# One accumulating DMA of two products in the first three rows of taps, with twelve product buffers

## The reference

```python
# layer 0: deformable attention, 8 heads, 4 points, 8 channels a head, q = x as tokens
v = q @ W_value + b_value
off = q @ W_off + b_off                       # per pixel, head and point: (dx, dy)
attn = softmax(q @ W_attn + b_attn)           # over the 4 points
# each point samples v bilinearly at (pixel position + off) of its own pixel
out = (sampled * attn).sum(points) @ W_out + b_out + q
# layer 1: binary 3x3 convolution of sign(x + move0), sign weights with a scale per channel,
# batch norm over the batch, + x, + move1, PReLU, + move2
```

## Time and profile before

| | |
|---|---|
| median of 3 runs | 95.57 us (95.44 to 96.04) |
| the profiled execution | 95.7 us |
| its span in the trace | 93.9 us |
| PE busy in the span | 76.6 us (82%) |
| DVE, POOL, ACT busy | 65.0, 51.0, 47.9 us |
| granted TensorE clock, mean | 0.953 |

### The profile page before, as it was taken

The page is one execution under the profiler, slowest core; times in us unless marked ns, Lnnn a source line. Parts: engine busy times, 40 slices in busy tenths (PEclk is TensorE's granted clock), DMA queues, the critical chain, the costliest instruction groups (busy, mean ns, idle before and its releaser), DMA issues.

```text
span 93.9 us, 1689 instructions
## 1 busy us (share of the span) xinstructions
PE 76.6 (82%) x648; PEld 33.0 (35%) x648; DVE 65.0 (69%) x81; ACT 47.9 (51%) x76; POOL 51.0 (54%) x47
## 2 busy tenths in 40 slices
PE   5999799879999999999997799999999999220000
PEld 4547074112246544333331355333333345010000
DVE  2624695995999664987973954997776408659930
ACT  2200899988689990399708950220000039419900
POOL 7920000059999999999998568899800000005000
PEclk9999999999999999999999999999999999996555
DMA  1998000000083083470924700910910000000095
GB/s 27 249 358 327 6 0 0 0 0 7 0 168 56 0 168 63 82 141 0 178 49 84 143 7 3 194 30 0 195 35 0 0 7 0 0 0 0 14 257 180
DMA packets 3209, 7.10 MB, mean 76 GB/s; under 512 B 512, under 2 KB 1024, under 8 KB 3200
## 3 DMA queue, kind: packets, MB, share of 16 engines
q0 software_dynamic: 1008, 3.67, 20.6%
q1 hardware_dynamic: 1904, 2.89, 9.8%
q10 hardware_dynamic: 288, 0.43, 1.5%
HBM read 2.27 MB, written 1.05 MB: 35 GB/s over the span
## 4 chain that ended last, share of the span: by engine, by line
PE 67%; ACT 15%; DVE 7%; issue 4%; POOL 3%; ACTq 1%; DVEq 0%; POOLq 0%
PE banks L431 27%; PE banks L451 23%; PE banks L444 4%; ACT tab L609 3%; ACT hat L614 3%; PE banks L483 3%; PE banks L501 3%; POOL ap L754 2%; ACT prod L734 2%; PE banks L404 2%; PE banks L396 2%; ACT prod L736 2%; DVE bns L957 1%; ACT sg L680 1%; ACT u L602 1%
## 5 line engine op out<-in xcount | busy, mean ns | idle before, releaser
L754 POOL TENSOR_TENSOR ap<-ays,hat 128x512 f32<-128x512 f32 x30 | 40.4, 1564 | 17.4 <-ACT ays L623 15.7
L850 DVE TENSOR_TENSOR prod<-banks,vpad 128x1024 f32<-128x1024 f32 (+1 forms) x33 | 38.6, 1187 | 11.7 <-PE banks L431 11.7
L431 PE MATMUL banks<-ap,cst 64*64 64x512 f32 x240 | 33.9, 596 | 1.3 <-DVE prod L850 1.1
L451 PE MATMUL banks<-prod,wo 64*64 64x512 f32 x200 | 27.8, 590 | 0.0
L431 PEld LDWEIGHTS banks<-ap,cst 64*64 64x64 f32 x240 | 10.1, 132 | 17.2 <-issue 9.4
L451 PEld LDWEIGHTS banks<-prod,wo 64*64 64x64 f32 x200 | 9.9, 133 | 11.5 <-issue 9.6
L779 POOL TENSOR_SCALAR prod<-prod,prm,st 128x512 f32<-128x512 f32 x2 | 1.5, 768 | 17.7 <-ACT st L728 17.7
L623 ACT ACTIVATE ays<-banks 128x512 f32<-128x512 f32 x8 | 4.7, 588 | 9.9 <-DVE banks L822 9.9
L609 ACT ACTIVATE tab<-u,cst 128x1024 f32<-128x1024 f32 x8 | 8.9, 1141 | 0.2
L680 ACT ACTIVATE sg<-banks,st 128x512 bf16<-128x512 f32 x2 | 1.3, 687 | 14.9 <-PE banks L451 14.9
L614 ACT ACTIVATE hat<-tab 128x1024 f32<-128x1024 f32 x8 | 8.3, 1050 | 0.1
(11 more groups left out here) (81 smaller groups left out, 74.0 us busy)
## 6 DMA issues: line engine op xcount, KB each, us to landing
prod<-prod POOLq DMA_DIRECT2D x7, 512.0 KB, 4.8
xs<-x_dram SPq DMA_DIRECT2D x3, 256.0 KB, 4.9
out_dram<-prod SPq DMA_DIRECT2D x4, 128.0 KB, 2.6
out_dram<-prod SPq DMA_DIRECT2D x2, 256.0 KB, 2.6
wcf<-w_conv_dram SPq DMA_DIRECT2D x1, 288.0 KB, 5.2
wab<-w_abs_dram SPq DMA_DIRECT2D x1, 288.0 KB, 5.2
xs<-x_dram ACTq DMA_DIRECT2D x1, 256.0 KB, 4.1
cst<-const_dram SPq DMA_DIRECT2D x1, 227.0 KB, 5.0
```

The lines of the kernel that those rows point to most:

```text
L431: mm = pe.matmul(ps_w[t % 2][rows_out, g, :], sel_of(g)[rows_in, rows_out], weights_at(t)[rows_in], start=True, stop=True)
L451: mm = pe.matmul(ps_out[g][rows_out], wo[rows_in, rows_in], source[rows_in, g, :], start=False, stop=last, skip_group_check=True)
L754: pool.tensor_tensor(ap[:, j % RAP, :], ays[:, t // TAPS % RY, :], hat[:, yh, 0, kx, :], ALU.mult).then_inc(s_ap, 1)
L850: nc.vector.tensor_tensor(by_half_row(prod[:, t % PR, g, :]), by_half_row(ps_w[t % 2][:, g, :]), v_window(g, yh, ky, kx), ALU.mult).then_i ...
```

## The change

In rows 0, 1 and 2 (`SUMMED_WHOLE`) one DMA now adds the two products of columns 2 and 3 onto those of columns 0 and 1: two slots of the ring onto two slots, 8 KB in each partition, 1 MB in all. It stands in POOL's list after weight 4(n+1)+3 and waits for product 4n+3. PE projects two units for such a row, both sums. Rows 3 to 6 keep their DMA of 512 KB and their three units, row 7 its four, so there are 3 x 2 + 4 x 3 + 4 = 22 units. The ring has PR = 12 buffers. `s_s2` has four semaphores, one for each row modulo 4. Where each unit is projected is written out in `UNITS_AT`.

```diff
--- before.py
+++ after.py
@@ -35,6 +35,7 @@
 
 ROWS = YH * TAPS
 SUMMED = range(ROWS - 1)
+SUMMED_WHOLE = range(3)
 DVE_COLUMNS = [2] + [0] * (ROWS - 1)
 GPSIMD_LINES = (0, 1)
 ORDER = (1, 0, 2, 3)
@@ -138,7 +139,7 @@
         RA, RAP = 3, 4
         a = sb("a", [P, RA, HALF])
         ap = sb("ap", [P, RAP, HALF])
-        PR = 8
+        PR = 12
         prod = sb("prod", [P, PR, G, HALF])
         over_sum = sb("over", [P, 2 * YH])
         overt = sb("overt", [P, 2, HALF])
@@ -209,7 +210,7 @@
         s_ap = sem("gpsimd_tap_weights_ready")
         s_w = sem("spread_ready")
         s_p = sem("products_ready")
-        s_s2 = [sem("even_pair_sums_ready"), sem("odd_pair_sums_ready")]
+        s_s2 = [sem(f"sums_ready{k}") for k in range(4)]
         s_acc = sem("units_projected")
         s_ov1 = sem("over_abs")
         s_ov = sem("over_ready")
@@ -323,20 +324,25 @@
 
             return t + 1 + (g if t == NT * YH - 1 else 0)
 
-        def units_of(n):
-
-            first = TAPS * n
-            if n == ROWS - 1:
-                return [("tap", t) for t in range(first, first + TAPS)]
-            return [("tap", first + 2), ("tap", first + 3), ("sum", n)]
-
-        UNITS_AFTER = {6: [("tap", 2), ("tap", 3)], 7: [("sum", 0)], 17: [("tap", 15), ("sum", 3)], 18: [], 20: [],
-                       21: [("tap", 18), ("tap", 19)], 31: [("tap", 28), ("tap", 29)]}
-        for n in range(2, ROWS):
-            for column in range(3):
-                UNITS_AFTER.setdefault(TAPS * n + column, units_of(n - 1)[column:column + 1])
-        UNITS = [unit for n in range(ROWS) for unit in units_of(n)]
-        UPPER_UNITS = sum(len(units_of(n)) for n in range(TAPS))
+        def sums_of(n):
+
+            return 2 if n in SUMMED_WHOLE else 1
+
+        def unit_of(t):
+
+            n, column = divmod(t, TAPS)
+            return ("sum", t) if n in SUMMED and column < sums_of(n) else ("tap", t)
+
+        def is_added(t):
+
+            n, column = divmod(t, TAPS)
+            return n in SUMMED and sums_of(n) <= column < 2 * sums_of(n)
+
+        UNITS_AT = {9: [0], 10: [1], 13: [4], 14: [5], 16: [14], 17: [15, 8], 18: [9, 12], 21: [18, 19], 22: [16], 24: [22],
+                    25: [23], 26: [20], 28: [26], 29: [27], 30: [24], 31: [28, 29]}
+        UNITS_AFTER = {t: [unit_of(k) for k in UNITS_AT[t]] for t in UNITS_AT}
+        UNITS = [unit for t in sorted(UNITS_AFTER) for unit in UNITS_AFTER[t]] + [unit_of(30), unit_of(31)]
+        UPPER_UNITS = UNITS.index(unit_of(12)) + 1
 
         def units_done(unit, g=G - 1):
 
@@ -462,11 +468,11 @@
                     pe.wait_ge(s_carry, 2)
                 last = unit in (UNITS[UPPER_UNITS - 1], UNITS[-1])
                 if kind == "sum":
-                    pe.wait_ge(s_s2[n % 2], 16 * (n // 2 + 1))
-                    source = prod[:, TAPS * n % PR]
+                    row = n // TAPS
+                    pe.wait_ge(s_s2[row % 4], 16 * (row // 4 + 1))
                 else:
                     pe.wait_ge(s_p, products_done(n, 0))
-                    source = prod[:, n % PR]
+                source = prod[:, n % PR]
                 mm = project_image(source, 0, last)
                 if unit == UNITS[-1]:
                     mm.then_inc(s_acc, 1)
@@ -755,16 +761,17 @@
 
             def pair_sum(n):
 
-                t = TAPS * n
-                pool.wait_ge(s_p, products_done(t + 1, G - 1))
-                pool.dma_start(prod[:, t % PR], prod[:, (t + 1) % PR], accum_op=ALU.add).then_inc(s_s2[n % 2], 16)
+                k = sums_of(n)
+                into = TAPS * n % PR
+                pool.wait_ge(s_p, products_done(TAPS * n + 2 * k - 1, G - 1))
+                pool.dma_start(prod[:, into:into + k], prod[:, into + k:into + 2 * k], accum_op=ALU.add).then_inc(s_s2[n % 4], 16)
 
             weight(2)
             weight(3)
             for n in range(ROWS - 1):
                 for column in range(TAPS):
                     weight(TAPS * (n + 1) + column)
-                    if column == 1:
+                    if column == 2 * sums_of(n) - 1:
                         pair_sum(n)
                 if n == 0:
                     pool.wait_ge(s_rec, 2)
@@ -836,14 +843,11 @@
                     dve.wait_ge(s_vlow, 2)
                 if t >= PR:
                     old = t - PR
-                    if old // TAPS in SUMMED and old % TAPS < 2:
+                    if is_added(old):
                         n = old // TAPS
-                        if old % TAPS == 0:
-                            dve.wait_ge(s_acc, units_done(("sum", n)))
-                        else:
-                            dve.wait_ge(s_s2[n % 2], 16 * (n // 2 + 1))
+                        dve.wait_ge(s_s2[n % 4], 16 * (n // 4 + 1))
                     else:
-                        dve.wait_ge(s_acc, units_done(("tap", old)))
+                        dve.wait_ge(s_acc, units_done(unit_of(old)))
                 dve.wait_ge(s_w, t + 1)
                 both = slice(0, G)
                 for g in ([both] if t < NT * YH - 1 else [slice(g, g + 1) for g in range(G)]):
```

## The result

The changed kernel is slower: 97.80 us, the median of 4 executions (97.38 to 98.92), against 95.50 us for the kernel before; the ratio is 1.021 [1.018, 1.024]. The forecast was 96.3 us, and its range ended at 97.6. The profiled execution takes 97.66 us with a span of 95.9 us, against 95.7 and 93.9, so 2.0 us have to be found. Executions more than 1.5% slower than the fastest of their kernel count in no ratio.

What follows compares the result with a forecast made beforehand. PE was taken as the bound, POOL hardly behind; 2.6 us from three units and 1.4 from the hole and smaller gaps stood against 4.6 of waits, 0.7 later unrounded: 96.3 us from 95.57, range 94.9 to 97.6.

Steps and rivals of the forecast that it cites:

- Case A: PE waits for the larger DMA at sums 0 and 4 (1.6 and 0.6 us), giving 96.3 us; chance 0.62.
- the hole at spread 20: PE stood 1.07 us waiting for product 18; hiding that product behind sums 9 and 12 would close it.
- The doubling of the data phase: A second 512 KB adds 2.75 us at 189 GB/s, so 1 MB lands 7.25 us after issue.
- B: Second half of the transfer nearly free, 2.65 us at 396 GB/s: 94.1 us, or 94.7 by the skill's fit; chance together 0.13.
- C: POOL's hold per DMA grows with bytes, 1.8 us not 0.9, delaying weights and later DMAs: 97.2 to 98.1 us; chance 0.18.
- D: PE, half busy from 28.7 to 34.6 us, falls to half clock, 1.7 us a block: 98 to 100 us; chance 0.04.
- the DMA of row 3 ... its data go behind those of row 2 (47.3) and land at 50.4: Row 3's DMA, issued at 43.3, queues behind row 2's and lands before sum 12 needs it at 51.2.
- both landings had under 1 us to spare: Rows 2 and 3 land at 47.7 and 50.4, sums 8 and 12 come at 48.6 and 51.2; slower DMAs delay the end.
- the twelve buffers cost nothing: The larger product ring is worth nothing, as each product's slot is free several us before it is needed.
- Forecast 0.7: Spread 20 starts at 52.9 instead of 52.19, so the kernel ends 0.7 us later.
- three units with 2.6 us: Three units removed from PE ahead of spread 20, 0.86 us each, 2.6 us in all.
- 4.6 us of waits: Waits at spreads 7, 8, 9, 13 (0.6, 0.65, 0.45, 0.7) and for DMAs at sums 0 and 4 (1.6, 0.6).

Runs made afterwards that it cites:

- early DMAs: Against the changed kernel: POOL issues the 1 MB DMAs two weights earlier, where the 512 KB ones stood; 95.87 us, 1.003 of the kernel before.
- early, row 2 later: Against the early DMAs: row 2's DMA stands one weight later in POOL's list, behind weight 14; 96.01 us, 0.999 of the kernel before.
- two halves: Against the changed kernel: two 512 KB DMAs, each with its own semaphore, replace each 1 MB DMA; 97.53 us, 1.015 of the kernel before.
- early, four waits: Against the early DMAs: four semaphore waits, satisfied long before, put back on DVE at products 8 to 11; 95.64 us, 0.997 of the kernel before.
- three units left out: Against the kernel before: products 3, 7 and 11 are never projected, all DMAs stay; 95.65 us, ratio 0.997.
- one unit moved: Against the kernel before: the sum of row 3 is projected behind spread 18, not 17; 95.31 us, 0.995, and in a second job 95.13 us, 0.991.
- two rows, four waits: Against the changed kernel: 1 MB DMAs only in rows 0 and 1, two weights earlier, four satisfied DVE waits, 23 units; 95.21 us, 0.995 of the kernel before.
- changed, four waits: Against the changed kernel: four satisfied semaphore waits added on DVE at products 8 to 11; 97.23 us, 1.017 of the kernel before.

## Why the prediction was wrong

In all profiles the span follows two numbers, when spread 20 starts and whether the end has its hole. The first four columns are differences to the kernel before, in us; "from first weight" is spread 20 counted from the start of POOL's first weight, which differs by up to 0.6 us between executions; "rest" is span less spread 20. The last two are the start of product 18 behind that of spread 18 (1.59 before) and the wait at the last DVE instruction (0.24 before).

| kernel | spread 20 | from first weight | span | rest | product 18 | last wait |
|---|---|---|---|---|---|---|
| changed | +1.26 | +1.14 | +2.0 | +0.74 | 1.18 | 0.63 |
| changed, again | +0.88 | +1.11 | +1.5 | +0.6 | 1.17 | 0.63 |
| early DMAs | -0.57 | -0.39 | +0.1 | +0.7 | 1.19 | 0.63 |
| no DMA for row 3 | +1.10 | +1.19 | +1.8 | +0.7 | 1.19 | 0.63 |
| before, 12 buffers | -0.37 | -0.35 | +0.3 | +0.7 | 1.18 | 0.63 |
| early, row 2 later (97.52 us) | +1.06 | +0.77 | +1.7 | +0.6 | 1.18 | 0.63 |
| two halves | +1.20 | +1.37 | +1.8 | +0.6 | 1.17 | 0.63 |
| early, four waits | -0.05 | -0.15 | -0.1 | 0.0 | 1.60 | 0.24 |
| three units left out | -0.08 | -0.23 | +0.1 | +0.2 | 1.59 | 0.24 |
| one unit moved | -1.32 | -1.03 | -1.3 | 0.0 | 1.61 | 0.24 |
| one unit moved, again | -0.84 | -1.00 | -0.8 | 0.0 | 1.61 | 0.24 |
| two rows, four waits | -0.22 | -0.38 | -0.2 | 0.0 | 1.59 | 0.24 |
| changed, four waits | +1.14 | +1.24 | +1.0 | -0.1 | 1.59 | 0.24 |

**The mechanism was right, its price was not.** Case A has PE waiting for the larger DMA at sum 0, and it does, 1.33 us; sum 0 and sum 4 start within 0.07 and 0.21 us of the forecast. At sum 4 PE hardly waits (0.6 us was forecast): spread 13 ends 0.2 us later than said, and the DMA lands 0.2 us earlier. The three units are gone and the hole at spread 20 with them. The doubling of the data phase (7.25 us to landing) was measured as 7.1 and 7.2 us for rows 0 and 1. The early DMAs show that this landing, at this place in the list, is the cause of the loss ahead of spread 20: 1.5 us come back by their issue alone, counted from the first weight.

**The rivals.** B, the second half nearly free, is false: 5.2 us of data, not 2.65. The Trainium skill's fit ("DMA: Bandwidth & Descriptors", Anatomy of one DMA) would have it land an estimated 4.4 us after issue and the trace disagrees, with 7.1; the Trainium skill's rule of two reads for one write ("Collectives: The Full Stack", The bandwidth ceiling) agrees with 200 against 396 GB/s. C, POOL held for longer, is false, as POOL's timeline of the changed kernel shows:

```profile
29.27 5.20 POOL L760 TENSOR_TENSOR ap<-ays,hat 128x512 f32<-128x512 f32 x4
34.22 1.10 POOL L767 DMA_DIRECT2D prod<-prod  x1
34.82 4.25 POOL L760 TENSOR_TENSOR ap<-ays,hat 128x512 f32<-128x512 f32 x3
```

The weights before the DMA end at 29.27 + 5.20 = 34.47 and the three behind it at 39.07: 4.6 us, of which three weights are 3.7, so the hold is 0.9 us for 1 MB as for 512 KB. D is false: over the whole stretch from 27.8 to 54.5 us the clock is at 1.00, its upper level, though PE is busy for 23.05 of 26.7 us.

**Two terms were mis-sized, and these are the steps that failed.** The first is the step "the DMA of row 3 ... its data go behind those of row 2 (47.3) and land at 50.4", with row 2 landing at 47.7 and sum 8 needing it at 48.6. Row 2 landed at 49.07. In this profile the data do not queue one behind the other at no cost. Row 3's DMA lands 7.9 us after issue (51.6), where 512 KB alone needs 4.5 to 5.1, and row 2's after 8.4 us, where it needs 7.6 with row 3's left out and row 0's needs 7.1; row 2's is issued at 40.63, not 40.2, too. The sum waits 0.51 us, with the matmuls' run-out 0.7 on the path. From sum 4 that gives 41.44 + 13 x 0.865 + 0.7 = 53.4 against the forecast 52.9. The forecast had said that both landings had under 1 us to spare, and left this out of the price. Without row 3's DMA the wait is gone. Repeating the kernel moves it to sum 12, and so does the run with four waits (0.60 us): in both row 2 takes 7.7 and 7.6 us, as alone, and row 3 7.9 and 8.0, 0.8 to 0.9 us more than the 7.1 of the forecast. Whether the engines mix the two or serve them in turn with a slow end is thus open; that the pair costs PE 0.5 to 0.6 us of wait is in all three.

The second is "the twelve buffers cost nothing". They cost 0.6 to 0.7 us behind the taps. This appears in all seven profiles with twelve buffers alone, and in none of the seven in which DVE has the waits of eight buffers or four others in their place. The same two groups part at product 18, where the pause stands in the second and is missing in the first: it is moved, and in the changed kernel it is moved from a place where it would be hidden to one where it is not. So it goes with four instructions of DVE's program, which is shown; why the length of the program sets the place of the pause, and why the output DMA takes 0.4 us more in the same cases, is open. Forecast 0.7 + 0.6 for the pair in flight + 0.7 for the end give the 2.0 us.

**And the gain was sized too high.** The forecast credits three units with 2.6 us and then finds 4.6 us of waits against this and the hole. Leaving the units out with nothing added brings 0.08 us at spread 20 (0.23 from the first weight), so there was next to nothing to gain ahead of the sum of row 2, full as PE was the earlier trace rows. The windows showed PE busy all the time, and did not show that POOL's issue of the next DMA would take its place at once. Of what was tried, the only part of the stretch that was worth anything by itself was the hole at spread 20, and one line of `UNITS_AFTER` closes it.

## What to carry to other kernels

Before work is taken from a full engine, ask for each landing and each foreign result behind it at what time it comes if the engine is early: work that is removed ahead of such a point is worth only what that point lets through, and a run that leaves the work out prices this. A larger DMA is paid in time from issue to landing, so it must be issued earlier by what it grows, and of two in flight at least one lands later than it would alone. Look also for pauses that are hidden today, since a change far away can move one to a place where it is paid. Try the reorder that fills the hole you can see first; here it beat a change of a whole stage.

## What the runs showed of the hardware

Four instructions more or less in DVE's program, none of which has to wait, decide where a pause of 0.4 us stands: at product 18, which starts 1.6 or 1.2 us behind its spread, or some 40 us later at the last instruction, with a hole of 0.24 or 0.63 us. With the hole goes the landing of the 256 KB output DMAs, 2.6 or 3.0 us. The cause is open.

An accumulating DMA within SBUF moved 189 to 202 GB/s in its data phase in rows 0 and 1 and held POOL for 0.9 us at 512 KB and at 1 MB alike. Alone, 1 MB landed 7.0 to 7.2 us after issue in rows 0 and 1 and 7.6 in row 2; with the next DMA 3.1 to 5.6 us behind, row 2's landed after 7.5 to 9.4 us.

With the one unit moved, the span is 92.6 to 93.4 us in 23 of 24 executions against some 93.9 before, 0.9 us less, but the medians of the time fell by only 0.4 and 0.7 us: the part around the span, 1.8 us in most executions of the other kernels, is 2.4 to 3.1 us in 11 of these 24. The kernel before has 2.1 to 2.9 us there in 18 of its 84 executions beside the experiments, so it is not peculiar to the moved unit. What does this is open.
